# Segment maxima of the attention scores: the mask is added by VectorE from a stored list, not by TensorE from a matmul

## The chip, the cores and the metric

The kernel runs on one core of a Trainium2 chip. The metric is the device time of one execution in microseconds (us). TensorE (PE in the rows) multiplies, VectorE (DVE), ScalarE (ACT) and GpSimd (POOL) work on elements, SyncE (SP) issues most of the DMAs.

## What is computed

Four graph networks run one after the other on the same 3125 nodes and 100,000 edges. What matters here is the first, and in it the loop over four layers. For each layer:

```
Q = ln(h @ Wq);  K = ln(h @ Wk)
score = (Q[src] * K[dst]).sum(-1) + 0.1 * (edge_attr * Q[src][:, :40]).sum(-1) + logm[dst]
smax  = segment_max(score, src)
es    = exp(min(score - smax[src], 20))
denom = segment_sum(es, src)
aggi  = segment_sum((es / (denom[src] + 1e-10)) * (h[dst] @ Wm), src)
h     = ln(h + leaky([h, aggi] @ Wu))
```

Ahead of the layers the same edges pass a gate once (`gate = mlp(edge_attr) + dot(emb[src], adapt emb[dst])`, messages `gate * h[dst] * weight`, summed by `src`).

## The kernel before

Edges were sorted into NB = 25 blocks by source: block i holds the edges whose source is one of the 128 nodes of block i, in KT = 38 tiles of 128 edges. For every tile there is a one-hot list of its sources (`hot_s`, edges by nodes) and its transpose (`hotT_s`, nodes by edges), in fp8, likewise for destinations (`hot_d`, `hotT_d`). The gate's stage (`gate_edges`) makes these lists and stores them to HBM (`rows_src`, `rows_src_t`, `rows_dst`, `rows_dst_t`). The layers' edge stage (`attend`, run four times, 25 blocks each) loads them again for each block.

**The gate's stage** runs over 25 blocks of Q = 7 units. VectorE makes the one-hot lists of the next block in eight chunks, destinations and sources in turn (L1392; a source chunk has 8, 12, 12 and 6 tiles), TensorE transposes them four tiles at a time into PSUM (`turn_hot`, L1290), ScalarE casts them from PSUM into `hotT_s` or `hotT_d` (`copied`, L1347). In the same unit TensorE gathers rows for the current block (`rows`, L1305 and L1307), ScalarE multiplies the embeddings (`emb_in`, L1356), VectorE forms the message (`message`, L1401 to L1409), GpSimd splits it (L1262, L1264), and TensorE sums it (L1317). Every engine's order is written out by hand. In ScalarE's, the casts of a unit stand ahead of its `emb_in`. SyncE's queue stores the lists of a block once all of its casts are done.

**The layers' edge stage** runs over 25 blocks of Q = 4 units of 10, 10, 9 and 9 tiles, several blocks deep. In each unit, in this order on TensorE: the keys and queries of its tiles (`keys`, L1578, L1580), in unit 1 also the turned scores (`turn_scores`, L1588) and the maxima spread over the edges (`maxima`, L1612), then two or three groups of `lay` with `values` (L1622) and `total` (L1633) between them. Ten groups of `lay` make up a block, nine of 4 tiles and one of 2. A group builds in one PSUM bank a table of 128 nodes by up to 512 edges: a first matmul (L1599) puts 0 where the edge belongs to the node and -2^100 where not (`off`, a 128 by 128 constant, times `hotT_s`), then one matmul per tile (L1602) adds the edge's score to every node's row (`sel` times `rows`; in three bf16 parts, so that their sum is exact). VectorE takes the maximum over each row (`top`, L1727). Two PSUM banks take turns, so TensorE starts group x only when VectorE has finished group x - 2.

VectorE's order in a unit: `add` (L1750, unit 1), `scores` (L1709, L1712), `divide` (L1720 to L1722, unit 0), `shifted` (L1744, L1746, unit 1), the unit's two or three `top`, and in unit 0 `largest` (L1734 to L1738). ScalarE takes the scores' rows (L1665), weighs the values (L1688) and copies the keys (L1672), GpSimd adds the attributes (L1536) and splits the values (L1543, L1545). SyncE's queue has for each block i, in this order: `first(i)` (L1498, L1499, waits until the values of block i - 4 are done), `attributes(i)` (L1504) and `last(i - 3)` (L1509, the `hot_s` that `total` needs).

## Time and profile before

| | us |
|---|---|
| median of 3 runs (lowest to highest) | 5786.9 (5772.91 to 5797.48) |
| the profiled execution | 5777.92 |
| its span, first to last instruction | 5776.3 |
| PE busy in the span | 4309.7 (75%) |
| DVE busy | 3791.9 (66%) |
| POOL busy | 2681.4 (46%) |
| ACT busy | 2250.1 (39%) |

Mean granted TensorE clock: 0.816 of full speed. A busy time is the union of an engine's instructions; idle time of an engine that isn't the bottleneck costs nothing. The gate's stage lies from about 1200 to 1866 us, the layers from about 1900 to 4157 us, of them the four edge stages some 430 us each and the rest in smaller stages between them. "Idle before" in a row is time in which the engine waited for the releaser named behind it.

### The profile page before, as it was taken

Reading aid. Unit: us, or ns where it says so; the run is one execution under the profiler, and the core shown is the slowest. Engines: PE = TensorE matmul, PEld = TensorE weight load, DVE = VectorE, ACT = ScalarE, POOL = GpSimd, SP = SyncE. Lnnn points to the kernel's source line nnn. Section 1 sums busy time; section 2 is a strip of 40 time slices with the busy share of each in tenths; the row PEclk is TensorE's granted clock in tenths of the full one; section 3 lists DMA queues with packets and bytes.
Section 4 is the critical chain, followed back from the end, with each engine's and each line's share of the span. In section 5 each row is a group of like instructions: output and inputs, shape, how many; then the busy total and the mean of one; then the engine's idle time right before and its main releaser. Section 6 shows DMA issues by size and latency. Waiting matters only on the chain. (4 is left out here: it accounts for less than half of the span.)

```text
span 5776.3 us, 186815 instructions
## 1 busy us (share of the span) xinstructions
PE 4309.7 (75%) x79576; PEld 3592.7 (62%) x79576; DVE 3791.9 (66%) x7925; ACT 2250.1 (39%) x7746; POOL 2681.4 (46%) x2702
## 2 busy tenths in 40 slices
PE   7999994046666499759976997599757845877887
PEld 4555552035555388748874887488735733877786
DVE  6888875079998588657765785687576446545244
ACT  3333331046666255435543554355401424101310
POOL 2777777756666177517751775277520510000000
PEclk7666665569998699869987998799877977988897
DMA  9322223167775344234423442344255434000000
GB/s 352 74 73 74 70 68 74 42 150 197 195 201 166 113 161 165 92 109 167 154 92 120 157 154 92 123 154 165 80 88 196 158 106 134 2 9 4 4 4 10
DMA packets 488184, 656.80 MB, mean 114 GB/s; under 512 B 316480, under 2 KB 370372, under 8 KB 484117
## 3 DMA queue, kind: packets, MB, share of 16 engines
q1 hardware_dynamic: 450965, 595.00, 32.7%
q0 software_dynamic: 33856, 48.44, 3.4%
q8 instruction: 645, 10.57, 0.7%
q14 instruction: 222, 1.82, 0.1%
q10 hardware_dynamic: 2496, 0.98, 0.1%
HBM read 464.16 MB, written 180.09 MB: 112 GB/s over the span
## 5 line engine op out<-in xcount | busy, mean ns | idle before, releaser
L299 POOL DMA_INDIRECT edges<-sb_bk_rec,sb_bk_pos x782 | 784.8, 1004 | 323.7 <-issue 234.0
L1688 ACT ACTIVATE sb_at_val<-banks,sb_at_prob 128x49 f32<-128x49 f32 x3800 | 776.0, 326 | 189.7 <-PE banks L1622 183.3
L1727 DVE TENSOR_REDUCE sb_at_tops<-banks 128x1 f32<-128x512 f32 x1000 | 652.5, 661 | 279.1 <-PE banks L1602 276.7
L1578 PE MATMUL banks<-sb_near,sb_at_hotT_d 128*128 128x49 bf16 x11100 | 610.3, 184 | 74.0 <-DVE sb_at_key L1709 44.5
L1536 POOL TENSOR_TENSOR sb_at_key<-sb_at_key,sb_at_attr 128x400 f32<-128x400 f32 (+1 forms) x400 | 371.8, 930 | 581.1 <-ACT sb_at_key L1672 489.9
L1580 PE MATMUL banks<-sb_queryp,sb_at_hotT_s 128*128 128x49 bf16 x11400 | 624.5, 185 | 12.8 <-issue 12.3
L1578 PEld LDWEIGHTS banks<-sb_near,sb_at_hotT_d 128*128 128x128 fp8e4 x11100 | 560.3, 96 | 79.1 <-issue 69.3
L1580 PEld LDWEIGHTS banks<-sb_queryp,sb_at_hotT_s 128*128 128x128 fp8e4 x11400 | 559.5, 96 | 15.7 <-issue 15.7
L1543 POOL TENSOR_TENSOR sb_at_val<-sb_at_val 128x490 f32<-128x490 f32 (+1 forms) x400 | 387.4, 968 | 68.9 <-ACT sb_at_val L1688 67.4
L1672 ACT COPY sb_at_key<-banks 128x490 f32<-128x490 f32 (+1 forms) x400 | 225.3, 563 | 462.9 <-PE banks L1580 460.6
L1545 POOL TENSOR_TENSOR sb_at_val<-sb_at_val 128x490 f32<-128x490 f32 (+1 forms) x400 | 386.6, 966 | 31.4
L1622 PE MATMUL banks<-sb_near,sb_at_hotT_d 128*128 128x49 bf16 x11100 | 358.5, 186 | 34.3 <-ACT sb_at_val L1688 22.6
L1602 PE MATMUL banks<-sb_at_rows,sb_sel 114*128 114x128 bf16 x3800 | 379.0, 220 | 1.2 <-issue 1.2
L1599 PE MATMUL banks<-sb_at_hotT_s,sb_off 128*128 128x512 fp8e4 x1000 | 369.4, 369 | 7.3 <-issue 4.5
L1602 PEld LDWEIGHTS banks<-sb_at_rows,sb_sel 114*128 114x128 bf16 x3800 | 297.0, 97 | 116.1 <-issue 9.2
L1622 PEld LDWEIGHTS banks<-sb_near,sb_at_hotT_d 128*128 128x128 fp8e4 x11100 | 331.7, 97 | 43.1 <-ACT sb_at_val L1688 29.1
L1633 PE MATMUL banks<-sb_at_val,sb_at_hot_s 128*128 128x147 bf16 x3800 | 342.3, 237 | 11.9 <-issue 9.1
L1709 DVE TENSOR_TENSOR sb_at_key<-banks,sb_at_key 128x490 f32<-128x490 f32 (+1 forms) x400 | 253.1, 633 | 143.5 <-POOL sb_at_key L1536 143.5
L1262 POOL TENSOR_TENSOR sb_gt_msg<-sb_gt_msg 128x245 f32<-128x245 f32 (+1 forms) x175 | 239.8, 1370 | 189.9 <-DVE sb_gt_msg L1409 189.2
L1633 PEld LDWEIGHTS banks<-sb_at_val,sb_at_hot_s 128*128 128x128 fp8e4 x3800 | 281.1, 101 | 14.4 <-issue 10.7
L2902 PE MATMUL banks<-sb_conv_parts,sb_C 128*128 128x144 bf16 x3750 | 249.3, 232 | 30.8 <-DVE sb_conv_parts L2852 30.8
L2902 PEld LDWEIGHTS banks<-sb_conv_parts,sb_C 128*128 128x128 bf16 x3750 | 247.6, 101 | 31.9 <-DVE sb_conv_parts L2852 31.9
(692 smaller groups left out, 10166.0 us busy)
## 6 DMA issues: line engine op xcount, KB each, us to landing
sb_at_attr<-attr SPq DMA_DIRECT2D x100, 760.0 KB, 7.5
sb_at_hotT_s<-rows_src_t SPq DMA_DIRECT2D x100, 608.0 KB, 3.9
sb_at_hot_s<-rows_src SPq DMA_DIRECT2D x100, 608.0 KB, 8.6
sb_at_hotT_d<-rows_dst_t SPq DMA_DIRECT2D x100, 592.0 KB, 5.9
edges<-sb_pad SPq DMA_DIRECT2D x95, 460.0 KB, 7.0
sb_gt_rec<-edges SPq DMA_DIRECT2D x25, 1748.0 KB
sb_we_hotT<-rows_dst_t SPq DMA_DIRECT2D x52, 592.0 KB, 5.8
attr<-sb_gt_rec SPq DMA_DIRECT2D x25, 760.0 KB, 13.2
```

What stands on the lines that cost most here:

```text
L299: pool.indirect_dma_start(list1, bass.IndirectOffsetOnAxis(pos[:, t:t + 1], 0), rec[:, k, j, :], None).then_inc(sent[k], 16)
L1536: pool.tensor_tensor(key[:, u % 2, 0:n, 0:RBF], key[:, u % 2, 0:n, 0:RBF], attr[:, i % 2, a:b, :], ALU.add).then_inc(s_key, 1)
L1543: pool.tensor_tensor(x[:, 0:n, 1, :], x[:, 0:n, 0, :], halves(0), ALU.subtract).then_inc(s_rest, 1)
L1545: pool.tensor_tensor(x[:, 0:n, 2, :], x[:, 0:n, 1, :], halves(1), ALU.subtract).then_inc(s_split2, 1)
L1578: pe.matmul(ps[:, 0, H1 * j:H1 * j + H1], where, what, start=(n == 0), stop=(n == 2))
L1580: ins = pe.matmul(ps[:, 1 + u % 2, H1 * j:H1 * j + H1], hotT_s[:, i % 4, k, :], queryp[:, i, n, :], start=(n == 0), stop=(n == 2))
L1602: ins = pe.matmul(bank[:, P * j:P * j + P], sel[:, k, :], rows[:, i % 2, :], start=False, stop=(k == ks[-1]))
L1622: ins = pe.matmul(ps[:, 5, H1 * j:H1 * j + H1], where, what, start=(n == 0), stop=(n == 2))
L1633: ins = pe.matmul(ps[:, 6, 0:3 * H1], hot_s[:, i % 2, k, :], high(val[:, v % VB, j].rearrange("p n f -> p (n f)")), start=(k == 0), stop=( ...
L1688: ins = act.mul(val[:, v % VB, j, 0, :], ps[:, 5, H1 * j:H1 * j + H1], prob[:, i % 2, k:k + 1])
L1727: dve.tensor_reduce(tops[:, i % 2, g:g + 1], ps[:, 3 + x % 2, 0:P * len(RG[g])], AX, ALU.max).then_inc(s_top, 1)
L2902: return pe.matmul(ps[:, d % AHEAD, 0:3 * H], C[:, s, P * d:P * d + P], rows(s), start=(s == 0), stop=(s == NB - 1))
```

## The change

TensorE's mask matmul goes from `lay`: each tile's matmul now starts and ends its own accumulation. The mask becomes a stored list, `others` (bf16, 128 nodes by 38 x 128 edges for each block, 1216 KB): 0 where the edge belongs to the node, -2^100 where not. ScalarE makes it in the gate's stage from `hotT_s` (Identity with scale 2^100 and bias -2^100), one activation behind the last cast of each source chunk, four per block. SyncE's queue stores it to HBM behind `hotT_d`. In the layers' edge stage SyncE's queue loads it for block i - 1 behind the attributes of block i and ahead of `last(i - 3)`, into one of two buffers. VectorE's `top` becomes one `tensor_tensor_reduce`: it adds the list to the scores in PSUM, writes the sum to a scratch buffer in SBUF (`left`, f32) and the row's maximum to `tops`.

```diff
 # gate_edges
+    LAST_S = {max(x for x, (t, _, _) in enumerate(TURN) if t == n): (a, b) for n, (side, a, b) in enumerate(MAKE) if side == "s"}
+    others, minus_big = m.sb("gt_others", [P, 2, KT, P], BF16), m.sb("gt_minus_big", [P, 1])
...
                 sp.dma_start(lists["hotT_d"][i], flat(hotT_d, i % 2)).then_inc(s_outt[i % 2], 16)
+                sp.wait_ge(s_others, len(LAST_S) * (i + 1))
+                sp.dma_start(lists["others"][i], flat(others, i % 2)).then_inc(s_outt[i % 2], 16)
...
                 act.copy(hotT[:, i % 2, ks[0]:ks[-1] + 1, :],
                          ps[:, y % 2, 0:P * len(ks)].rearrange("p (k e) -> p k e", e=P), saturate=False).then_inc(s_copied, 1)
+                if x in LAST_S:
+                    a, b = LAST_S[x]
+                    act.wait_ge(s_copied, y + 1)
+                    act.activation(others[:, i % 2, a:b, :], hotT_s[:, i % 2, a:b, :], ACT.Identity, bias=minus_big[:], scale=BIG).then_inc(s_others, 1)
...
 # attend
+            def apart(i):
+                if i >= 2:
+                    sp.wait_ge(s_top, NR * (i - 1))
+                sp.dma_start(flat(others, i % 2), lists["others"][i]).then_inc(s_others[i % 2], 16)
...
                     first(i)
                     attributes(i)
+                if i - 1 < NB:
+                    apart(i - 1)
                 if i >= 3:
                     last(i - 3)
...
                 ks, bank = RG[g], ps[:, 3 + x % 2, :]
-                n = P * len(ks)
-                pe.matmul(bank[:, 0:n], off[:], hotT_s[:, i % 4, ks[0]:ks[-1] + 1, :].rearrange("p k e -> p (k e)"), start=True,
-                          stop=False)
                 for j, k in enumerate(ks):
-                    ins = pe.matmul(bank[:, P * j:P * j + P], sel[:, k, :], rows[:, i % 2, :], start=False,
-                                    stop=(k == ks[-1]))
+                    ins = pe.matmul(bank[:, P * j:P * j + P], sel[:, k, :], rows[:, i % 2, :], start=True, stop=True)
                 ins.then_inc(s_laid, 1)
...
             def top(i, g):
                 x = NR * i + g
+                n, ks = P * len(RG[g]), RG[g]
                 dve.wait_ge(s_laid, x + 1)
-                dve.tensor_reduce(tops[:, i % 2, g:g + 1], ps[:, 3 + x % 2, 0:P * len(RG[g])], AX, ALU.max).then_inc(s_top, 1)
+                if g == 0:
+                    dve.wait_ge(s_others[i % 2], 16 * (i // 2 + 1))
+                if x >= 2:
+                    dve.wait_ge(s_top, x - 1)
+                dve.tensor_tensor_reduce(left[:, x % 2, 0:n], ps[:, 3 + x % 2, 0:n],
+                                         others[:, i % 2, ks[0]:ks[-1] + 1, :].rearrange("p k e -> p (k e)"), 1.0, -BIG,
+                                         ALU.add, ALU.max, tops[:, i % 2, g:g + 1]).then_inc(s_top, 1)
```

## Rows read from the trace of the kernel before

**Rows 1.** By stage: length, busy PE, PEld, DVE, ACT, POOL; clock, DMA share, GB/s.
```profile
2107.02:2296.53 189.51, 183.28 (x5144) 170.47 (x5141) 152.47 (x320) 111.54 (x485) 135.27 (x144) 1.00 0.43 161
1458.00:1562.00 104.00, 68.98 (x1360) 60.93 (x1358) 96.43 (x165) 71.34 (x232) 69.33 (x61) 0.92 0.74 198
```

**Rows 2.** ScalarE's timeline, layers' stage: start, duration; [idle before], at blocks 1 and 12.
```profile
2107.02 0.27 ACT L1665 COPY sb_at_rows<-banks 114x128 bf16<-114x128 bf16 x1 [1.46 <-PE banks L1588]
...
2296.53 0.27 ACT L1665 COPY sb_at_rows<-banks 114x128 bf16<-114x128 bf16 x1 [1.46 <-PE banks L1588]
```

**Rows 3.** Waits from 2107.02 to 2296.53: total us, times, longest.
```profile
DVE sb_at_tops L1727 <- PE banks L1602: 30.0, 60, 2.2
PE banks L1580 <- issue: 2.5, 3, 1.2
PE banks L1578 <- issue: 2.1, 1, 2.1
PE banks L1622 <- issue: 1.6, 4, 0.6
```

**Rows 4.** TensorE's timeline in one unit of the layers' stage.
```profile
2229.05 0.38 PE L1599 MATMUL banks<-sb_at_hotT_s,sb_off 128*128 128x512 fp8e4 x1
2229.27 0.39 PE L1602 MATMUL banks<-sb_at_rows,sb_sel 114*128 114x128 bf16 x4
2229.49 0.77 PE L1622 MATMUL banks<-sb_near,sb_at_hotT_d 128*128 128x49 bf16 x24
...
2230.62 0.85 PE L1633 MATMUL banks<-sb_at_val,sb_at_hot_s 128*128 128x147 bf16 x10
```

**Rows 5.** Groups by shape, VectorE, whole span: busy us, mean ns | idle before.
```profile
L1727 DVE TENSOR_REDUCE sb_at_tops<-banks 128x1 f32<-128x512 f32 x900 | 611.2, 688 | 257.1 <-PE banks L1602 254.7
...
L1709 DVE TENSOR_TENSOR sb_at_key<-banks,sb_at_key 128x490 f32<-128x490 f32 x200 | 131.6, 658 | 129.2 <-POOL sb_at_key L1536 129.2
...
L542 DVE TENSOR_TENSOR_SCAN sb_bk_along<-sb_bk_reset,sb_bk_spill 128x400 bf16<-128x400 bf16 x49 | 48.7, 994 | 1.7
```

**Rows 6.** The same view of ScalarE.
```profile
L2664 ACT ACTIVATE sb_nodes<-sb_C 128x3200 bf16<-128x3200 bf16 x12 | 34.4, 2870 | 20.2 <-PEq L86 19.8
...
L970 ACT ACTIVATE sb_nr_sq<-sb_nr_qk 128x480 f32<-128x480 f32 x20 | 12.0, 602 | 0.6
...
L3233 ACT ACTIVATION_READ_ACCUMULATOR sb_nodes<-banks,sb_wide_cols 108x1 f32 x52 | 10.1, 194 | 0.0
```

**Rows 7.** ScalarE's timeline in the gate's stage: casts of source lists, then embedding products.
```profile
1505.94 0.59 ACT L1347 CAST sb_gt_hotT_s<-banks 128x512 fp8e4<-128x512 f32 x1 [0.28 <-PE banks L1290]
1507.07 1.00 ACT L1356 ACTIVATE sb_gt_emb<-banks,sb_gt_rec 128x32 f32<-128x32 f32 x5 [0.55 <-PE banks L1307]
...
1515.44 1.07 ACT L1347 CAST sb_gt_hotT_s<-banks 128x512 fp8e4<-128x512 f32 x2 [0.24 <-PE banks L1290]
1516.80 1.18 ACT L1356 ACTIVATE sb_gt_emb<-banks,sb_gt_rec 128x32 f32<-128x32 f32 x6 [0.28 <-PE banks L1307]
...
1523.19 1.74 ACT L1347 CAST sb_gt_hotT_s<-banks 128x512 fp8e4<-128x512 f32 x3 [0.20 <-PE banks L1290]
1525.29 1.00 ACT L1356 ACTIVATE sb_gt_emb<-banks,sb_gt_rec 128x32 f32<-128x32 f32 x5 [0.36 <-PE banks L1307]
```

**Rows 8.** VectorE's timeline there: its first operation behind those products.
```profile
1508.11 0.32 DVE L1401 TENSOR_TENSOR sb_gt_prod<-banks,sb_gt_emb 128x160 f32<-128x160 f32 x1
...
1518.63 0.35 DVE L1401 TENSOR_TENSOR sb_gt_prod<-banks,sb_gt_emb 128x192 f32<-128x192 f32 x1
...
1526.81 0.31 DVE L1401 TENSOR_TENSOR sb_gt_prod<-banks,sb_gt_emb 128x160 f32<-128x160 f32 x1
```

**Rows 9.** VectorE's waits from 1300 to 1800 us.
```profile
DVE sb_gt_prod L1401 <- ACT sb_gt_emb L1356: 22.3, 49, 1.3
```

**Rows 10.** DMA issues of the page: count, KB each, median us to landing.
```profile
sb_at_hot_s<-rows_src SPq DMA_DIRECT2D x100, 608.0 KB, 8.6
```

**Rows 11.** The DMA queue's timeline: the block's last load is issued.
```profile
2213.92 0.53 SPq L1509 DMA_DIRECT2D sb_at_hot_s<-rows_src  x1
```

More of the change, by code:

```diff
@@ L1202, in gate_edges @@
     names = ["near", "at", "hot", "turned", "copied", "rows", "emb", "prod", "msg", "rest", "split2", "sum", "added",
-             "link", "second", "back"]
+             "link", "second", "back", "minus", "others"]
     with stage(nc, "gate", *names, *[f"rec{k}" for k in range(HB)], *[f"outh{k}" for k in range(HB)], "outt0", "outt1",
@@ L1206, in gate_edges @@
             block, s_near, s_at, s_hot, s_turned, s_copied, s_rows, s_emb, s_prod, s_msg, s_rest, s_split2, s_sum,
-            s_added, s_link, s_second, s_back, *dmas):
+            s_added, s_link, s_second, s_back, s_minus, s_others, *dmas):
         s_rec, s_outh, s_outt, s_outa, s_far = dmas[0:3], dmas[3:6], dmas[6:8], dmas[8:11], dmas[11:15]
@@ L1247, in _ @@
             for n in range(2):
-                sp.wait_ge(s_outt[n], 32 * ((NB - 1 - n) // 2 + 1))
+                sp.wait_ge(s_outt[n], 48 * ((NB - 1 - n) // 2 + 1))
             sp.wait_ge(s_back, 16)
@@ L1343, in copied @@
                 if x == 0 and i >= 2:
-                    act.wait_ge(s_outt[i % 2], 32 * (i // 2))
+                    act.wait_ge(s_outt[i % 2], 48 * (i // 2))
                     act.wait_ge(s_rows, Q * (i - 1))
@@ L1357, in emb_in @@
                 ins.then_inc(s_emb, 1)
+            act.wait_ge(s_minus, 1)
             for q in range(Q):
@@ L1415, in add @@
                                   ).then_inc(s_added, 1)
+            dve.memset(minus_big[:], -BIG).then_inc(s_minus, 1)
             link(dve.tensor_tensor(tops[:], c["ident"][:, 0:KT], c["ident"][:, KT:2 * KT], ALU.add))
@@ L1441, with attend @@
 K1, KH = H1, 2 * H1
-def attend(nc, c, ps, m, lists, table, near, queryp, dead, sel, off, acc, nmax, spill_dst):
+def attend(nc, c, ps, m, lists, table, near, queryp, dead, sel, acc, nmax, spill_dst):
     TAKE = [range(0, 10), range(10, 20), range(20, 29), range(29, KT)]
@@ L1468, in attend @@
     rows = m.sb("at_rows", [3 * KT, 2, P], BF16)
+    others, left = m.sb("at_others", [P, 2, KT, P], BF16), m.sb("at_left", [P, 2, 4 * P])
     tops = m.sb("at_tops", [P, 2, NR])
@@ L1477, in attend @@
     rings = [f"attr{k}" for k in range(2)] + [f"hots{k}" for k in range(2)] + [f"hotT{k}" for k in range(4)] + [
-        f"far{k}" for k in range(4)] + [f"near{k}" for k in range(Q)]
+        f"far{k}" for k in range(4)] + [f"others{k}" for k in range(2)] + [f"near{k}" for k in range(Q)]
     turned_bank = ps[:, 7, 128:192].bitcast(BF16)
@@ L1482, in attend @@
             s_prob, s_h, s_val, s_rest, s_split2, s_sum, s_added, s_link, *dmas):
-        s_attr, s_hots, s_hotT, s_far, s_near = dmas[0:2], dmas[2:4], dmas[4:8], dmas[8:12], dmas[12:]
+        s_attr, s_hots, s_hotT, s_far, s_others, s_near = dmas[0:2], dmas[2:4], dmas[4:8], dmas[8:12], dmas[12:14], dmas[14:]
         @block.sync
@@ L2524, in first_part @@
             near = t.sb("near", [P, NW, 3, KH], BF16)
-            attend(nc, c, ps, t, lists, table, near, queryp, dead, sel, off, acc, nmax, spill_dst)
+            attend(nc, c, ps, t, lists, table, near, queryp, dead, sel, acc, nmax, spill_dst)
         with ExitStack() as ctx0:
@@ L3466, in network @@
     lists = {"hot_s": nc.dram_tensor("rows_src", [NB, P, KT * P], F8).ap(),
+             "others": nc.dram_tensor("rows_others", [NB, P, KT * P], BF16).ap(),
              "hotT_s": nc.dram_tensor("rows_src_t", [NB, P, KT * P], F8).ap(),
```

## The prediction

> **What bounds the kernel now.** I read the table of busy times by stage first. In the layers' edge stage (the stretch from 2107.02 to 2296.53) TensorE is busy 183.3 of 189.5 us at clock 1.00 (the 2.4 GHz level), VectorE 152.5, GpSimd 135.3, ScalarE 111.5: TensorE sets the pace there [rows 1]. The two ends of the stretch are the same copy, eleven blocks apart, so a block takes 189.51 / 11 = 17.23 us [rows 2]. The waits say the same from the other side: VectorE waits for the laid-out scores, 30.0 us in 60 pieces, while TensorE waits 2.5 + 2.1 + 1.6 = 6.2 us, and for no engine ("issue") [rows 3]. What each would need by itself: TensorE (189.5 - 6.2) / 11 = 16.7 us a block, VectorE (189.5 - 30.0) / 11 = 14.5 us. So any time taken from TensorE counts, but only until VectorE's 14.5 us are reached, and the change puts work just there. In the gate's stage VectorE is busy 96.4 of 104 us, ScalarE 71.3, TensorE 69.0 at clock 0.92, with the DMA engines at a share of 0.74: VectorE sets that pace, and ScalarE isn't far behind it in the order of the work, since VectorE waited for it 22.3 us in 49 pieces within 500 us [rows 1, 9].
>
> **TensorE loses the mask matmul.** In the timeline of one unit the mask's matmul starts at 2229.05, the four tile matmuls behind it at 2229.27, and the next work at 2229.49 [rows 4]. The durations (0.38, 0.39) overlap, so the starts count: 0.22 us for the mask, 0.22 us for the tiles. Nine full groups and one of half the width make 9.5 x 0.22 = 2.1 us a block. TensorE's need falls from 16.7 to 14.6 us, and with the 6.2 / 11 = 0.6 us of its own waits to 15.2 us.
>
> **VectorE's reduce becomes an add with a reduce.** The trace has no such operation. What lies nearest is in two rows: the reduce over 512 elements from PSUM takes 688 ns, and an addition-like operation with one operand in PSUM, one in SBUF and its result in SBUF takes 658 ns for 490 elements, so some 22 elements more bring it to 0.68 us [rows 5]. The pass over the elements should therefore cost what the reduce costs. The maximum has to be brought out beside the sum. The only row for that is ScalarE's read of its accumulator, 194 ns for one element a partition, behind the activation that filled it [rows 6]. I bound the addition by 0 and 0.19 us each and take the middle, 0.1 us, as no row of VectorE decides it: 1.0 us a block. The far bound is the scan, the one two-operand operation here that carries a result from element to element: 994 ns for 400 elements, or 1.27 us for 512 [rows 5]; that is the third rival below. The extra waits in `top` (for the list once a block, for the maximum two groups back on its own engine) cost nothing while the list is there in time.
> The Trainium skill ("VectorE: DVE Perf Modes", section "Two Vector instructions with no wait between them") says that an operation which also writes out its accumulator is two instructions, the main one and an accumulator read. By that rule the sum keeps the second instruction at some price, without it nothing; no row here shows it for VectorE.
>
> **The new period.** VectorE's need becomes 14.5 + 1.0 = 15.5 us, TensorE's 15.2 us. VectorE is then the slightly later one, and its order has two heavy units of four (units 0 and 1 with `divide`, `largest`, `shifted`), in which TensorE, only two groups ahead, has to wait. I add 0.1 us for that: 15.6 us, or 1.6 us less than 17.23. Each of the four layers has 24 full periods; the rest is filling and draining. 96 x 1.6 = 154 us off. If the read costs nothing, TensorE decides at 15.2 us: 96 x 2.0 = 195 us off. With 0.19 us VectorE needs 16.4 us, with the 0.1 us 16.5: 96 x 0.7 = 70 us off.
>
> **ScalarE's four activations a block in the gate's stage.** An activation from SBUF takes 602 ns for 480 elements and 2870 ns for 3200, so (2870 - 602) / 2720 = 0.83 ns an element and 0.2 us ahead of them [rows 6]. Chunks of 1024, 1536, 1536 and 768 elements cost 1.05, 1.48, 1.48 and 0.84 us, 4.9 us a block, and about 0.1 us each for the wait on the cast just issued. ScalarE has the room (71.3 of 104 us), but they stand between the casts and the embedding products on which VectorE waits. Three of the four places are in the rows. The casts end at 1506.53, 1516.51 and 1524.93, and the products start at 1507.07, 1516.80 and 1525.29 [rows 7]. With 0.1 + 1.48, 0.1 + 1.05 and 0.1 + 1.48 us put between, they start at 1508.1, 1517.7 and 1526.5, later by 1.0, 0.9 and 1.2 us. VectorE's first use of them comes 0.04, 0.65 and 0.52 us behind their end (1508.07, 1517.98, 1526.29) [rows 7, 8], and it has its one-hots to make until then. So it is held up 1.0, 0.2 and 0.7 us; for the smallest chunk I take 0.2. That is 2.1 us a block, 24 x 2.1 = 50 us on the stage. The bounds: 20 us, if VectorE gets ahead in the other units, and 4.9 x 25 = 120 us if nothing of it is hidden.
>
> **The DMAs.** The store of 1216 KB a block and its load four times over are new. The layers' stage moved 161 GB/s at a share of 0.43 [rows 1], so 16 engines at that mix would move 374 GB/s, and 1216 KB (1.25 MB) take 3.3 us of them: the share goes to (0.43 x 17.23 + 3.3) / 15.6 = 0.69. In the gate's stage the same 3.3 us in a block of some 26 us (666 us of stage by 25) lift 0.74 to about 0.85. On SyncE's queue the new load stands ahead of `last`, which lands 8.6 us after its issue now [rows 10] and would at 8.6 + 3.3 + 0.5 for the longer queue = 12.4 us. It is issued at 2213.92 and first used by the `total` at 2230.62, 16.7 us later [rows 4, 11]; with a block 1.6 us shorter 15.1 us are left, 2.7 us more than it needs. The list itself lands before that and is wanted at about the same time. I put the DMAs at nothing: the 12.4 us hide beside the other work. If a load were late, it would hold up every block. The new wait in the queue (maxima of block i - 3 done) is met when VectorE has left unit 0, at most a unit after the keys that `attributes` waits for; behind it only `last` is queued.
>
> **The sum.** -154 + 50 = -104 us on the profiled span of 5776.3 us: 5672. The profiled execution took 5777.92 us, 9 below the median of 5786.9, so for the median 5787 - 104 = **5683 us**.
>
> **The rivals.**
> *The gate's stage takes back most of the gain.* ScalarE's work rises from 71.3 / 104 = 0.69 of the time to about 0.83, and it serves TensorE's transposes too, which already wait for its casts. With nothing hidden (+120) and the read at its dear end (-70) the sum is +50; with +95 and -105 it is about -10, 5777 us. For it: the embedding products are late already in 49 cases. Against it: in the rows two of three places have half a microsecond of room. Within half a per cent of no change.
> *The read costs nothing and ScalarE hides.* -195 + 25 = -170: 5617 us. For it: the reduce and the two-operand pass cost alike.
> *The fused operation is slow, and VectorE becomes the bound.* If it runs like the scan, 1.27 us for 0.69, a block costs VectorE 14.5 + 9.5 x 0.58 = 20.0 us, above 17.23: +2.8 x 96 + 50 = +319 us, 6106 us. It decides against the change from 14.5 + 9.5 x d > 17.23, d over 0.29 us, even with the gate's stage at nothing, and with its 50 us from d over 0.23 (0.5 us a block less). A milder form, d = 0.35, gives 17.9 us a block, +64 + 50: 5901 us. For it: only the scan shows feedback with two operands. Against it: the reduce feeds back too, at 688 ns for 512.
> The Trainium skill ("Vector Engine (DVE) Microarchitecture Reference", section "Points that are easy to get wrong") has it that a two-source operation whose sources are both in SBUF and not bf16 runs at half rate, for want of a port to read back its accumulator. Here one source is in PSUM and the other bf16, so by that rule it shouldn't; no row of this trace tells.
> *The change doesn't shorten TensorE's path*, since the tile matmuls were hidden behind the mask's stream: then nothing is gained and 50 us lost. The starts in the rows (0.22 us for each part) speak against it; it goes with the slow cases.
>
> **Chances.** The forecast 0.50, the cheap end 0.18, the gate's stage eating most of it 0.14, slow operation or late load 0.18 (half of it mild). The 80% range goes from 5595 (all of TensorE's time and a hidden ScalarE, -192) to 5830 (the dear read and an unhidden ScalarE, and a little of the mild slow form). A difference under 0.5% (29 us) is about what a measurement can't tell from no change: faster by more than that 0.74, within 0.09, slower 0.17.
>
> **What the profile after would show.** TensorE's group of mask matmuls gone from the layers; the copy of the rows every 15.6 us; `top` at 0.69 us and, if it is there, a row of a second operation near 0.1 us; VectorE's idle before it nearly gone, TensorE waiting for `sb_at_tops`. In the gate's stage ScalarE's four activations at 1.05 to 1.48 us, VectorE's wait for the embedding products up from 22 to some 60 us in 500, and the stage 50 us longer. The forecast falls if `top` takes over 0.9 us, if VectorE's or TensorE's waits name a DMA, or if the gate's stage grows by over 100 us.

## The result

The changed kernel takes 5981.37 us (median of 4 runs, 5965.08 to 5986.14), the kernel before beside it 5782.27 us: a ratio of 1.0337 (95% interval 1.0305 to 1.0368). It is 199 us slower, where 104 us faster was forecast. The two profiled spans differ by 5976.3 - 5776.3 = 200.0 us, and two stages hold all of it.

**The gate's stage.** The view of one tile gives the first and last start of ScalarE's embedding products (ns are min/median/max), of before:

```profile
L1356 ACT ACTIVATE sb_gt_emb<-banks,sb_gt_rec x950: 278/289/385, 1221.8 to 1865.6; 128x32 f32<-128x32 f32 x190
```

and of after, with ScalarE's four new activations a block:

```profile
L1364 ACT ACTIVATE sb_gt_emb<-banks,sb_gt_rec x950: 266/288/316, 1223.0 to 1902.0; 128x32 f32<-128x32 f32 x190
L1356 ACT ACTIVATE sb_gt_others<-sb_gt_hotT_s,sb_gt_minus_big x100: 934/1362/1577, 1208.2 to 1887.8; 128x1536 bf16<-128x1536 fp8e4 x50, 128x1024 bf16<-128x1024 fp8e4 x25, 128x768 bf16<-128x768 fp8e4 x25
```

The stage lasted 643.8 us and lasts 679.0: 35 us longer. VectorE's waits from 1300 to 1800 us, which answer to [rows 9]:

```profile
DVE sb_gt_prod L1410 <- ACT sb_gt_emb L1364: 41.5, 71, 1.3
```

**The layers' edge stage.** From the first copy of the turned scores to the last (24 blocks apart) the four layers took 408.0, 411.7, 410.8 and 410.0 us, in all 1640.5; now they take 450.2, 452.2, 449.2 and 455.7, in all 1807.3. That is 167 us more, and with the gate's 35 us the 200. The rows of after that answer to [rows 1] and [rows 2], for 18 blocks of the first layer (columns as there):

```profile
2097.12:2442.82 345.70, 282.72 (x8232) 278.49 (x8229) 249.70 (x703) 183.96 (x793) 220.55 (x234) 0.93 0.58 209
```

```profile
2097.12 0.27 ACT L1678 COPY sb_at_rows<-banks 114x128 bf16<-114x128 bf16 x1 [6.39 <-PE banks L1605]
...
2442.82 0.27 ACT L1678 COPY sb_at_rows<-banks 114x128 bf16<-114x128 bf16 x1 [6.07 <-PE banks L1605]
```

(2442.82 - 2097.12) / 18 = 19.21 us a block, where the same 18 blocks of before took 17.28 (and the eleven of [rows 2] 17.23). TensorE is busy less (282.7 of 345.7 us; 300.2 of 311.0 in the same 18 blocks of before) and VectorE no more (249.7 us; 249.5): the work of neither fills the block now. The granted clock is 0.93 where it was 1.00. The waits in that stretch, which answer to [rows 3]:

```profile
DVE sb_at_left L1745 <- PE banks L1616: 63.6, 65, 4.7
DVE sb_at_shift L1764 <- PE banks L1625: 21.7, 17, 3.7
PE banks L1635 <- issue: 21.0, 9, 4.3
PE banks L1595 <- issue: 20.2, 13, 3.5
PE banks L1597 <- issue: 18.0, 8, 3.5
PE banks L1616 <- issue: 3.7, 3, 1.5
```

VectorE does wait for TensorE, as before, and more. But TensorE waits for no engine and no list: 21.0 + 20.2 + 18.0 + 3.7 = 62.9 us are "issue", 3.5 us a block, in pieces of up to 4.3 us. Before, the same sum was 10.6 us in 18 blocks, 0.6 a block.

**VectorE's new operation is not the cause.** Its group, beside [rows 5], and two of them in the timeline:

```profile
L1745 DVE CUSTOM_DVE_ANT_0 sb_at_left<-banks,sb_at_others 128x512 f32<-128x512 f32 x900 | 609.0, 687 | 271.4 <-PE banks L1616 262.9 <-issue 1.6
```

```profile
2161.23 0.68 DVE L1745 CUSTOM_DVE_ANT_0 sb_at_left<-banks,sb_at_others 128x512 f32<-128x512 f32 x1
2161.84 0.08 DVE L1745 DVE_READ_ACCUMULATOR2_ANT sb_at_tops<- 128x1 f32 x1
2161.84 0.68 DVE L1745 CUSTOM_DVE_ANT_0 sb_at_left<-banks,sb_at_others 128x512 f32<-128x512 f32 x1
```

It takes 687 ns where the plain reduce took 688. The maximum is brought out by a second instruction of 0.08 us, which lies inside the next one's start: the two additions start 0.61 us apart. The second instruction is what the Trainium skill says ("VectorE: DVE Perf Modes", section "Two Vector instructions with no wait between them"), and the trace agrees; its price here is nothing.

**What TensorE waits for.** Four of its waits, in its own timeline of after:

```profile
2155.26 0.43 PE L1635 MATMUL banks<-sb_near,sb_at_hotT_d 128*128 128x49 bf16 x6 [4.34 <-issue]
...
2170.40 0.20 PE L1595 MATMUL banks<-sb_near,sb_at_hotT_d 128*128 128x49 bf16 x1 [0.85 <-issue]
...
2176.14 0.20 PE L1595 MATMUL banks<-sb_near,sb_at_hotT_d 128*128 128x49 bf16 x1 [1.74 <-issue]
...
2191.53 0.20 PE L1597 MATMUL banks<-sb_queryp,sb_at_hotT_s 128*128 128x49 bf16 x1 [2.03 <-issue]
```

The view of the DMA queues tells packets, MB and share by queue in a stretch. In the 7.5 us from 2145 to 2152.5 these were all:

```profile
q1 hardware_dynamic: 369, 2.28, 74.1%
q0 software_dynamic: 48, 0.08, 9.7%
q14 instruction: 1, 0.01, 0.3%
```

and in the half microsecond behind it there is one packet of 16 KB on the queue q8, which the page calls instruction:

```profile
q8 instruction: 1, 0.02, 12.1%
q1 hardware_dynamic: 5, 0.02, 9.5%
```

TensorE stood still from 2150.9 and went on at 2155.26. The packet itself takes about 1 us of one engine (12.1% of 16 engines in 0.5 us), as it does in the mean with the lists' traffic and without it (65 packets at 1.2% of 16 x 345.7 us here, 1.0 us each; 1.2 us each in experiment 7): it isn't slow, it comes late. Asked in steps of half a microsecond, the view puts the q8 packets at 2144.5, 2152.5, 2156.5, 2161.0, 2167.5, 2173.5, 2177.5, 2182.5 and 2189.0, and so on. Every issue wait of more than 0.8 us between 2150 and 2252 ends 2.2 to 2.9 us behind the start of the half microsecond in which such a packet ran:

| q8 packet at | TensorE goes on at | its wait, us |
|---|---|---|
| 2152.5 | 2155.26 | 4.34 |
| 2167.5 | 2170.40 | 0.85 |
| 2173.5 | 2176.14 | 1.74 |
| 2189.0 | 2191.53 | 2.03 |
| 2202.5 | 2204.95 | 1.14 |
| 2209.0 | 2211.87 | 2.42 |
| 2226.5 | 2228.72 | 2.48 |
| 2240.5 | 2243.36 | 1.09 |
| 2247.5 | 2250.09 | 2.67 |

Packets on that queue in the same 18 blocks, in before:

```profile
q8 instruction: 66, 1.08, 1.3%
```

and in after:

```profile
q8 instruction: 65, 1.06, 1.2%
```

That is 3.6 or 3.7 a block, and the counts fit TensorE's instructions: in after 8232 matmuls and 8229 weight loads (the first two counts of the busy times above), 16461 / 65 = 253 a packet, in before 8413 + 8410 = 16823, 16823 / 66 = 255. TensorE works through one in 311.02 / 66 = 4.7 us at the old pace and would in 15.6 / 3.6 = 4.3 us at the pace that was forecast. While a block's lists are loaded, they come 6 to 9 us apart.

What settles that these are the packets TensorE waits for is where in its stream it waits. From the end of one such wait to the start of the next one, the view of stretches counts its matmuls and weight loads (the first two counts behind the busy times):

```profile
2155.26:2170.35 15.09, 14.29 (x380) 14.18 (x380) 11.82 (x34) 9.52 (x43) 8.19 (x9) 0.83 0.56 192
2170.40:2176.10 5.70, 3.99 (x127) 3.88 (x127) 5.05 (x16) 2.75 (x12) 4.01 (x5) 1.00 0.58 199
2176.14:2191.50 15.36, 13.36 (x381) 13.24 (x381) 10.72 (x27) 7.75 (x33) 9.30 (x10) 0.89 0.69 257
```

That is 760, 254 and 762: with its waits on semaphores counted too, 768, 256 and 768, three packets, one and three. It is so in the whole trace of after: its four layers' edge stages have 133 issue waits of more than 0.8 us, and all 129 distances between neighbours of one stage are a multiple of 256 instructions, give or take one. In before it is so for all 25 distances between 29 such waits. Each of the 133 ends 2.2 to 2.5 us behind the start of a q8 packet. The DMA engines' mean share in slices of 1 us (tenths) shows the loads, of before from 2212 on:

```profile
DMA  0779999981000000000799999941000000004999
```

of after from 2150 on:

```profile
DMA  8310000000005999799996891000003999999999
```

Before, a block's loads fill 7 or 8 slices in a row with a share of 0.5 or more, after, 12; between them lie slices of no share, where a q8 packet such as that at 2156.5 has the engines to itself. So the reading is: TensorE's instructions come over the same DMA engines as the lists, they are late in a long stretch of list traffic, and the extra 1216 KB makes the stretch longer than what TensorE has in store (how much that is, no run measured). The experiments test that.

The Trainium skill ("Runtime: NRT & Kernel Launch", section "Instruction fetch mechanics") says that instructions are refilled in blocks of 16 KiB, 256 of them, over a DMA queue of the sequencer's own, and that this is mostly hidden. The packets and the distances agree with the first (65 packets of 1.06 MB, waits a multiple of 256 instructions apart), and the 3.5 us of waits a block speak against the second.

### The profile page after: what moved, and what is told of

The parts are those of the page before. It is cut to its first block and busy times, and to the rows that moved or that the text cites. A ratio compares the mean times of both kernels' runs of the same rounds, so it can differ in the third digit from the quotient of the medians.

```text
span 5976.3 us, 186953 instructions
## 1 busy us (share of the span) xinstructions
PE 4223.5 (71%) x78491; PEld 3627.4 (61%) x78576; DVE 3811.1 (64%) x8926; ACT 2373.2 (40%) x7846; POOL 2673.5 (45%) x2702
## 5 line engine op out<-in xcount | busy, mean ns | idle before, releaser
L1745 DVE CUSTOM_DVE_ANT_0 sb_at_left<-banks,sb_at_others 128x512 f32<-128x512 f32 x1000 | 649.8, 661 | 339.8 <-PE banks L1616 329.0
L1595 PE MATMUL banks<-sb_near,sb_at_hotT_d 128*128 128x49 bf16 x11100 | 656.0, 188 | 139.3 <-issue 88.9
L1597 PE MATMUL banks<-sb_queryp,sb_at_hotT_s 128*128 128x49 bf16 x11400 | 670.1, 189 | 100.3 <-issue 100.2
L1595 PEld LDWEIGHTS banks<-sb_near,sb_at_hotT_d 128*128 128x128 fp8e4 x11100 | 587.8, 99 | 150.6 <-issue 142.9
L1597 PEld LDWEIGHTS banks<-sb_queryp,sb_at_hotT_s 128*128 128x128 fp8e4 x11400 | 583.9, 98 | 104.8 <-issue 104.7
L1635 PE MATMUL banks<-sb_near,sb_at_hotT_d 128*128 128x49 bf16 x11100 | 384.4, 190 | 98.7 <-issue 69.7
L1635 PEld LDWEIGHTS banks<-sb_near,sb_at_hotT_d 128*128 128x128 fp8e4 x11100 | 356.5, 100 | 116.1 <-issue 79.5
L1616 PE MATMUL banks<-sb_at_rows,sb_sel 114*128 114x128 bf16 x3800 | 397.1, 229 | 40.3 <-issue 30.5
L1646 PE MATMUL banks<-sb_at_val,sb_at_hot_s 128*128 128x147 bf16 x3800 | 369.8, 250 | 2.4 <-POOL sb_at_val L1562 2.1
L1646 PEld LDWEIGHTS banks<-sb_at_val,sb_at_hot_s 128*128 128x128 fp8e4 x3800 | 307.9, 107 | 3.6 <-POOL sb_at_val L1562 3.2
L1616 PEld LDWEIGHTS banks<-sb_at_rows,sb_sel 114*128 114x128 bf16 x3800 | 245.4, 101 | 42.0 <-issue 26.9
L1725 DVE TENSOR_REDUCE sb_at_score<-sb_at_key 128x10 f32<-128x490 f32 (+1 forms) x400 | 255.4, 638 | 13.8
```

The source lines that it names most:

```text
L1595: pe.matmul(ps[:, 0, H1 * j:H1 * j + H1], where, what, start=(n == 0), stop=(n == 2))
L1597: ins = pe.matmul(ps[:, 1 + u % 2, H1 * j:H1 * j + H1], hotT_s[:, i % 4, k, :], queryp[:, i, n, :], start=(n == 0), stop=(n == 2))
L1616: ins = pe.matmul(bank[:, P * j:P * j + P], sel[:, k, :], rows[:, i % 2, :], start=True, stop=True)
L1635: ins = pe.matmul(ps[:, 5, H1 * j:H1 * j + H1], where, what, start=(n == 0), stop=(n == 2))
L1646: ins = pe.matmul(ps[:, 6, 0:3 * H1], hot_s[:, i % 2, k, :], high(val[:, v % VB, j].rearrange("p n f -> p (n f)")), start=(k == 0), stop=( ...
L1745: dve.tensor_tensor_reduce(left[:, x % 2, 0:n], ps[:, 3 + x % 2, 0:n], others[:, i % 2, ks[0]:ks[-1] + 1, :].rearrange("p k e -> p (k e)") ...
```

## The experiments

They ran on three chips, on which before took 5998 us (experiments 1 to 4), 6008 us (5 to 8) and 5773 us (9 to 12). The extra time of the first two lies ahead of the gate's stage (which starts at 1406 to 1422 us in their traces, at 1221 to 1223 in the others) and behind the layers (some 35 us); the layers' edge stages last the same on all. Ratios are to before on the same chip. Forecasts given in microseconds were made for before at 5782, and are read as ratios. The cuts of code leave out the waits that go with a load that is moved or left out.

### 1 and 2: the gate's stage alone, and with the load

```diff
 # e1: the gate's stage of the change, the layers of before
+                    act.activation(others[...], hotT_s[...], ACT.Identity, bias=minus_big[:], scale=BIG)
+                sp.dma_start(lists["others"][i], flat(others, i % 2))
 # e2: the same, and in the layers
+                if i - 1 < NB:
+                    apart(i - 1)
```

> The change's gate stage alone: ScalarE makes the list of 0 and -2^100 and SyncE's queue stores it; the layers are those of before (mask matmul and plain reduce; the list isn't loaded). Theory (the layers' loads do the harm): the gate's stage is about 35 to 55 us longer than before and the layers are unchanged: 5815 to 5845 us, ratio 1.006 to 1.010. Rival (the gate's stage is what made the kernel slower): most of the 200 us is here, above 5900 us.

> As the gate stage alone, and in the layers the list is loaded and waited for as in the change, but nothing reads it: the mask matmul and the plain reduce of before stay. Theory (each block's load lengthens the burst of DMA traffic behind which TensorE's own instructions wait to be fetched, which shows as issue waits): TensorE's issue waits grow from some 60 us to 200 us or more and the time is 150 to 350 us above the gate stage alone, so 5970 to 6180 us, slower than the change itself. Rival (VectorE's new operation does it): no more than 30 us above the gate stage alone.

The gate's stage alone: 1.0065 (1.0041 to 1.0089), its stage 679.3 us long, as in the change, and the layers at 17.30 us a block as before. With the load, which nothing reads: 1.0383 (1.0351 to 1.0416), at least about as slow as the change (the intervals overlap). TensorE does in it what it did before, mask matmul and all, and takes 350.66 / 18 = 19.48 us a block, with 36.6 us of issue waits:

```profile
2291.32:2641.98 350.66, 314.03 (x8413) 289.35 (x8411) 247.06 (x521) 182.86 (x793) 219.48 (x234) 0.96 0.56 206
```

So 3.2% come from the load alone, and VectorE's operation has no part in them. The waits are 1.4 us a block more than in before (2.0 for 0.6), of 2.2 us in all; the other 0.8 is TensorE's busy time (314.0 us for 300.2 on the same instructions), with the granted clock at 0.96 where it was 1.00. So the waits cost clock besides, with more work on TensorE than in the change.

### 3: two loads of the new list a layer

```diff
-                if i - 1 < NB:
+                if i - 1 < 2:
                     apart(i - 1)
```

> The change as it is, but of each layer's 25 loads of the list only the first two are issued, so that blocks 2 to 24 add the list of block 0 or 1 (their maxima are not the reference's). Theory (the load is the harm, the new operation costs what the reduce did): a block takes 15.2 to 15.8 us, TensorE's issue waits are back near 60 us, and the time is 5640 to 5700 us, below before. Rival (VectorE's operation, or its coupling to TensorE, is the bound): within 50 us of the change, 5930 us or more.

Measured 0.9989 (0.9976 to 1.0002). The load is worth 3.5% here too (1.0337 to 0.9989), but the forecast of 15.2 to 15.8 us a block and 60 us of issue waits was wrong: a block takes 16.86 us in the first layer, and TensorE's issue waits there are

```profile
PE banks L1595 <- issue: 17.5, 10, 2.4
PE banks L1635 <- issue: 6.3, 5, 2.0
PE banks L1616 <- issue: 3.9, 3, 1.6
PE banks L1597 <- issue: 2.1, 2, 1.9
```

29.8 us in 18 blocks, 1.7 a block against 0.6 before, with the same bytes as before. A faster TensorE uses up its instructions sooner, so what was enough at 17.3 us a block is no longer. Of the 2.1 us of the mask matmul only 17.30 - 16.86 = 0.4 us came through.

### 4: the load in quarters

```diff
             def apart(i):
-                if i >= 2:
-                    sp.wait_ge(s_top, NR * (i - 1))
-                sp.dma_start(flat(others, i % 2), lists["others"][i]).then_inc(s_others[i % 2], 16)
+                for p, (a, b) in enumerate(PARTS):
+                    if p == 0 and i >= 2:
+                        sp.wait_ge(s_top, NR * (i - 1))
+                    if p:
+                        sp.wait_ge(s_key, Q * i + p + 1)
+                    sp.dma_start(...).then_inc(s_others[4 * (i % 2) + p], 16)
```

> The change with each block's load of the list cut into four parts, issued behind the last load of the block and spaced by TensorE's progress (one part a unit of some 3.8 us) rather than in one burst; same bytes. Theory (the length of the burst without a gap is what starves the instruction fetch): issue waits fall to 60 to 130 us and the time to 5680 to 5800 us. Rival (it is the bytes moved, by load on the DMA engines or on memory, whenever they are moved): no better than 5930 us.

1.0285 (1.0255 to 1.0315), 19.21 us a block, 3.4 us of issue waits. By its numbers the rival would have won, but the experiment didn't do what it was made for: the keys' count stood higher than I had reckoned, the four parts were issued within 6.5 us, and they left the stretch as it was instead of parting it. In its slices, from 2329 on, the loads still fill 11 and 13 slices in a row (12 in the change):

```profile
DMA  4799999998961000000597799999599630000499
```

It tells only that smaller packets and a later place in the queue don't help by much.

### 5 and 6: all loads spaced, in the change and in before

```diff
                     first(i)
-                    attributes(i)
-                if i - 1 < NB:
-                    apart(i - 1)
-                if i >= 3:
-                    last(i - 3)
+                for slot, (loads, pieces) in enumerate([(["attr"], [0]), (["hots"], [1]), ([], [2, 3])]):
+                    sp.wait_ge(s_keys, min(Q * i - 1 + slot, U))
+                    if "attr" in loads and i < NB:
+                        attributes(i)
+                    if "hots" in loads and i >= 3:
+                        last(i - 3)
+                    if i - 1 < NB:
+                        for p in pieces:
+                            apart(i - 1, p)
```

> The change with all of the layers' loads spaced by TensorE's own progress: per block the two transposed lists, then a unit later the attributes and the first quarter of the new list, a unit later the source list and the second quarter, a unit later the rest. Same bytes, four stretches of some 2 to 3 us with gaps where there was one of 12 us. Theory (a long unbroken stretch of data starves the instruction fetch): the stretches are seen apart in the DMA's slices, issue waits fall below 1 us a block, a block takes 15.2 to 16.2 us, ratio to before 0.97 to 0.985. Rival (bytes alone count, wherever they lie): issue waits stay near 3 us a block and the ratio at 1.025 or more.

> The kernel before, with its own loads spaced in the same way and nothing else changed. Theory: its issue waits (0.6 us a block) shrink, ratio 0.990 to 1.000. Rival (bytes alone): 1.000.

The change with spaced loads: 1.0061 (1.0035 to 1.0087), 17.43 us a block, 34.0 us of issue waits in 18 blocks (1.9 a block; 3.5 in the change). Its slices from 2333 on:

```profile
DMA  0599999979933830047999995389834560056999
```

Stretches with a share of 0.5 or more are now 10, 1, 7, 3 and 2 slices long here, with short gaps between. The same bytes in shorter stretches took 2.7% off, so bytes alone aren't it; but it isn't the 15.2 to 16.2 us that I expected either, since at a mean share of 0.67 the gaps are short. Before with spaced loads: 0.9979 (0.9962 to 0.9997), 17.15 us a block, 0.5 us of issue waits, as forecast and hardly to be told from nothing: by this reading, TensorE's store of instructions nearly reached over the loads at before's pace.

### 7: no list traffic

```diff
-                    first(i)
-                    attributes(i)
+                    if i < 4:
+                        first(i)
+                    if i < 2:
+                        attributes(i)
+                if i - 1 < 2:
                     apart(i - 1)
-                if i >= 3:
+                if 3 <= i < 5:
                     last(i - 3)
```

> The change with each list and the attributes loaded only into the first filling of their buffers, so that later blocks work on old lists (the result is not the reference's) and TensorE has next to no data traffic beside its instruction fetch. Theory: issue waits near 0, a block takes 14.7 to 15.4 us, the layers' edge stages are some 190 us shorter than before, ratio 0.97 to 0.98. Rival (the issue waits are TensorE's own, from its shorter matmuls): they stay at 1.5 us or more a block and the ratio near 0.999, as with two loads of the new list.

0.9765 (0.9737 to 0.9792), the gate's 0.65% included. In the first layer, 18 blocks, the length and busy times, TensorE's waits, and the DMA queues:

```profile
2283.31:2559.59 276.28, 268.27 (x8233) 262.71 (x8230) 259.17 (x703) 183.35 (x792) 220.71 (x235) 1.00 0.05 9
```

```profile
PE banks L1627 <- DVE sb_at_mparts L1760: 4.3, 18, 0.2
PE banks L1607 <- DVE sb_at_sparts L1737: 3.7, 18, 0.2
```

```profile
q0 software_dynamic: 864, 1.36, 2.9%
q8 instruction: 65, 1.06, 1.7%
```

Not one issue wait is left, the clock is 1.00, and each block takes 15.3 or 15.4 us, 15.35 in the mean in all four layers. The instruction packets are the same 65, in the mean 276.28 / 65 = 4.25 us apart. Against before, the four layers' edge stages are 1640.5 - 1468.1 = 172 us shorter. Block time and ratio lie in the forecast, and the rival, that the waits come from TensorE's shorter matmuls themselves, is out: its instructions are those of the change. This is the kernel that the prediction described, and it exists only without the lists' traffic (it works on old lists).

### 8: the activation behind the embedding products

```diff
-                if x in LAST_S:
-                    act.wait_ge(s_copied, y + 1)
-                    act.activation(others[...], ...)
 ...
                 emb_in(u)
+                for x in made:
+                    if x in LAST_S:
+                        list_of(j, x)
```

> The spaced loads, and in the gate's stage ScalarE makes the list's part behind the unit's embedding products instead of ahead of them. Theory (the gate's stage grew because VectorE waits for products that stand behind the new activations): the stage is 25 to 45 us shorter than with the activations ahead, ratio 0.005 to 0.007 below the spaced kernel. Rival (the stage grew by the store's DMA traffic): no difference.

1.0065 (1.0045 to 1.0085) against 1.0061 for experiment 5: no difference. The gate's stage is 675.5 us long against 682.9, 7 us and not 25 to 45, and in the other traces with the same gate's stage it is 678.9 to 682.5. VectorE still waits 39.0 us for the products from 1500 to 2000 us, now in 48 longer pieces instead of 47.4 us in 85. So the order on ScalarE isn't what made the stage longer, or not for the most part; the room that ScalarE has lost comes back as a wait wherever the work stands, or the store does it. Which of the two, I haven't tried. TensorE's fetch is not it: its matmuls have 2.8 us of issue waits in that stage of after and 3.8 in before.

### 9 and 10: the mask from the one-hot list that is there

```diff
 # divide: 256 is added to the scores
-                link(dve.tensor_tensor(sp[:, 0, :], score[:, i % 3, :], dead[:, i, :], ALU.add))
+                link(dve.scalar_tensor_tensor(sp[:, 0, :], score[:, i % 3, :], UP, dead[:, i, :], ALU.add, ALU.add))
 # top
+                dve.tensor_tensor_reduce(left[:, x % 2, 0:n], ps[:, 3 + x % 2, 0:n],
+                                         hotT_s[:, i % 4, ks[0]:ks[-1] + 1, :].bitcast(mybir.dt.uint8)..., 1.0 / 56.0, 0.0,
+                                         ALU.mult, ALU.max, tops[:, i % 2, g:g + 1])
 # largest: and taken off the stored maximum again
-                link(dve.tensor_scalar(nm, mp[:, 0:1], 1.0, None, ALU.mult))
+                link(dve.tensor_scalar(nm, mp[:, 0:1], UP, None, ALU.add))
 # e10 besides: the loads spaced as in experiment 6
```

> The mask matmul taken from TensorE as in the change, but without a new list: 256 is added to the scores, VectorE multiplies them by the one-hot list that is in SBUF for TensorE anyway (its fp8 ones read as the byte 56, the product scaled by 1/56) and takes the maximum, 0 standing for the edges of other nodes. No new traffic and nothing new in the gate's stage. Theory: a block takes 16.5 to 16.9 us as with two loads of the new list, issue waits about 1.5 us a block, ratio 0.991 to 0.994. Rival (bytes read by VectorE cost more than bf16): the reduce takes over 0.75 us and the ratio is 1.00 or more.

> The same with the layers' loads spaced by TensorE's progress: the two transposed lists, a unit later the attributes, a unit later the source list. Theory: issue waits under 0.7 us a block, a block takes 15.5 to 16.2 us, ratio 0.975 to 0.985, below both kernels. Rival (spacing helps only where there is much traffic): as without spacing, 0.991 to 0.994.

The mask matmul is gone, no list is made, stored or loaded, and VectorE's operation reads the one-hots' bytes (1.0 is 56 there, hence 1/56): the scores, made positive by 256, are multiplied by 0 or 1 as the maximum is taken. Unspaced: 0.9916 (0.9900 to 0.9931), inside the forecast, though a block takes 17.05 to 17.27 us and not 16.5 to 16.9; the four layers take 1614.1 us, 26 less than before, with 1.9 us of issue waits a block. Spaced: **0.9838 (0.9822 to 0.9855), 5687.4 us against 5772.8**, faster than both kernels. Its first layer's lengths and busy times, TensorE's waits in it, and its operation in the groups of VectorE:

```profile
2058.72:2351.29 292.57, 269.49 (x8233) 264.89 (x8230) 251.50 (x704) 182.01 (x793) 220.85 (x235) 0.99 0.49 171
```

```profile
PE banks L1585 <- issue: 11.4, 9, 2.1
PE banks L1625 <- issue: 6.5, 6, 2.1
PE banks L1606 <- issue: 3.5, 3, 1.4
```

```profile
L1733 DVE CUSTOM_DVE_ANT_0 sb_at_left<-banks,sb_at_hotT_s 128x512 f32<-128x512 f32 x900 | 603.1, 686 | 146.4 <-PE banks L1606 140.9 <-issue 0.2
```

16.25 us a block, clock 0.99, 22.3 us of issue waits in 18 blocks (1.2 a block, where I had expected under 0.7). The four layers take 1542.7 us, 98 less than before. 0.9 us a block are still left to the 15.35 of experiment 7.

### 11 and 12: the change again, and half of its loads

```diff
 # e12
-                if i - 1 < NB:
+                if i - 1 < NB and (i - 1) // 2 % 2 == 0:
                     apart(i - 1)
```

> The change itself, beside the other runs on one chip. Both theories: ratio 1.030 to 1.037.

> The change with the new list loaded for blocks 0, 1, 4, 5, 8, 9 and so on alone; the others add an older one (the result is not the reference's). Theory (each burst that is longer starves TensorE for itself): blocks with the load take some 19 us, blocks without 17, ratio 1.013 to 1.020, half way between two loads (0.999) and the change. Rival (a threshold of traffic): as two loads or as the change.

The change again: 1.0345 (1.0324 to 1.0366). With half of the new list's loads: 1.0171 (1.0150 to 1.0192), half way between 0.9989 and 1.0345, 18.07 us a block and 2.4 us of issue waits (3.5 with all, 1.7 with two). No threshold shows in these three points. The blocks with the load are the long ones: the load comes for two blocks and stays away for two, and block times, taken by their place in that round of four, are 19.0, 17.6, 16.9 and 18.4 us in the mean of the four layers (18.8 to 19.4 in the change).

All of it side by side, first layer, 18 blocks from the fifth copy to the 23rd:

| kernel | ratio | us a block | issue waits a block | clock | DMA GB/s |
|---|---|---|---|---|---|
| before | 1 | 17.28 | 0.6 | 1.00 | 160 |
| the change | 1.034 | 19.21 | 3.5 | 0.93 | 209 |
| e1 gate only | 1.007 | 17.30 | 0.6 | 1.00 | 160 |
| e2 gate and load | 1.038 | 19.48 | 2.0 | 0.96 | 206 |
| e3 two loads | 0.999 | 16.86 | 1.7 | 0.97 | 164 |
| e12 half the loads | 1.017 | 18.07 | 2.4 | 0.94 | 188 |
| e4 quarters | 1.029 | 19.21 | 3.4 | 0.94 | 209 |
| e5 change, spaced | 1.006 | 17.43 | 1.9 | 0.95 | 232 |
| e6 before, spaced | 0.998 | 17.15 | 0.5 | 1.00 | 162 |
| e7 no lists | 0.977 | 15.35 | 0.0 | 1.00 | 9 |
| e9 one-hots | 0.992 | 17.27 | 1.9 | 0.96 | 161 |
| e10 one-hots, spaced | 0.984 | 16.25 | 1.2 | 0.99 | 171 |

In e9 the first layer happened to be the slowest (its others 17.05 to 17.22). In the change a block without its issue waits would take 19.21 - 3.49 = 15.72 us, close to the 15.35 with no traffic. What is left goes with the clock, as far as the rows tell: in the timeline of after, three matmuls of 49 columns take 0.30 us behind the long wait that ends at 2155.26 and 0.23 to 0.24 us from 2162.50 on, and the clock is 0.83 from 2155.26 to 2170.35 (the row above).

## Why the prediction was wrong

**TensorE's loss of the mask matmul** (2.1 us a block; need 14.6 us, 15.2 with its own waits): right in kind, 0.3 us too much. In experiment 7 TensorE is busy 268.27 / 18 = 14.9 us a block, where its need before was 16.7: 1.8 us came.

**VectorE's operation** (0.68 us and 0 to 0.19 for the read): right in the pass, 687 ns, and too dear in the read. The range began with the right end, 0. So VectorE didn't become the later engine: in experiment 7 TensorE is busy 268.3 of 276.3 us and sets the pace. That its 15.35 us lie so near the forecast's 15.6 (172 us off the layers for 154) is partly luck: the 15.6 held 1.0 us of reads that cost nothing, and the 15.35 hold none of the 0.6 us of issue waits that TensorE's 15.2 were reckoned with.

**VectorE's lateness in its heavy units**: 0.1 us was added, and experiment 7 leaves TensorE 4.3 + 3.7 us of waits for VectorE in 18 blocks, 0.4 a block. They stand before the turned scores (L1607) and the maxima (L1627), not before the tables of `lay`, and are inside the 15.35.

**ScalarE's activations**: 1.05, 1.48 and 0.84 us forecast, 1.15, 1.58 and 0.94 us measured (1575 ns for 1536 elements, 1148 for 1024, 935 for 768). 50 us were forecast for the stage and 35 came. The mechanism given for it, products held up behind the new activations, didn't hold by itself: with the activations behind the products the stage was 3 to 7 us shorter, not 35.

**The DMAs**: here the prediction failed. "I put the DMAs at nothing: the 12.4 us hide beside the other work" was reckoned against the first user of each list, and those users are indeed not late. The landing times came nearly as forecast (the page of after; count, KB, us to landing; 12.4 us was the forecast for the second):

```profile
sb_at_others<-rows_others SPq DMA_DIRECT2D x100, 1216.0 KB, 10.9
sb_at_hot_s<-rows_src SPq DMA_DIRECT2D x100, 608.0 KB, 11.7
```

and in the 18 blocks of the rows above no engine's wait names a list. What was left out is another user of the same DMA engines that isn't in the kernel's text: TensorE's instruction fetch. The sum had 6.2 us of its issue waits [rows 3] and carried them over as a constant, 0.6 us a block. They were the sign of it. They grow with the length of the load stretches (0.6 to 2.0 us a block, experiment 2) and with TensorE's pace (0.6 to 1.7, experiment 3), and the change raised both: 3.5. In the layers -154 us became +167. Experiment 7 has the change's instructions there without the lists' traffic, and lies 167 + 172 = 339 us below it: that is what the traffic costs through TensorE's waits and clock. The term put at nothing, with the 0.6 us a block (58 us) that was carried over, stood for these 339 us; the other terms were 18 us (the layers' pace) and 15 us (the gate's stage) too dear.

**The rivals.** None was this one. "Slow operation or late load" had 0.18, but its mechanism was VectorE's price; the sentence that a late load would hold up every block had the right engines and the wrong waiter. The chance of slower, 0.17, was too low, because the one resource that the change loads most, the DMA engines, was checked only for deadlines.

**What the profile after should have shown**: `top` at 0.69 us with a second operation near 0.1 us, and VectorE's waits for the products up to about 60 us (41.5), came. The copy every 15.6 us and TensorE waiting for `sb_at_tops` did not: TensorE's issue waits took that place, which the list of signs didn't hold.

**What stays open.** That TensorE waits for its instructions rests on the places of its waits, a multiple of 256 instructions apart, on their ends behind the packets of one queue, and on their going when the list traffic goes. The number of TensorE's instructions was never changed by itself. Why a packet comes 6 to 9 us after the last one under load (asked for late, or held up in a queue), how far ahead TensorE fetches, and whether an order of the queues could let a packet pass, no run tells. Nor was the gate's 35 us split between ScalarE's time and the store.

## What to carry to other kernels

Before moving work off TensorE at the price of DMA traffic, look at TensorE's waits for "issue" and at the instruction queue's packets: this kernel, unrolled into many short matmuls, lives on a steady fetch, and both a longer stretch of data (experiment 2) and a faster TensorE (experiment 3) starved it. Reckon traffic not only against the deadline of its own reader but for how long it fills the engines without a gap, and space the loads by TensorE's own progress. A mask that is already in SBUF in another form (here one-hots, with an offset that makes the scores positive) costs no traffic at all: it was worth 0.8% by itself and 1.6% with the loads spaced, where the new list lost 3.4%.

## What the runs showed of the hardware

- The fused add-and-maximum over 512 elements, one operand in PSUM and one bf16 in SBUF, takes 687 ns, the same as the plain maximum; with a byte operand, 686 ns. Bringing the maximum out is an instruction of 0.08 us that costs the next one nothing (0.61 us from start to start).
- TensorE's instructions come in packets of 16 KB, 3.6 for a block. They came 4.25 us apart in the mean with no list traffic, and 6 to 9 us apart during a stretch of list loads, though one takes about 1 us either way. TensorE's 133 issue waits of more than 0.8 us in the change's layers lie a multiple of 256 instructions apart and end 2.2 to 2.5 us behind the start of a packet.
- The granted clock fell with TensorE's waits: 0.93 with 3.5 us of waits in 19.21 us, 1.00 with none in 15.35 us, on the same instructions. In experiment 2 it fell to 0.96 with the instructions of before, which ran at 1.00.
- Two chips took 3.9 and 4.1% longer than the third for the kernel before (5998 and 6008 against 5773 us), 185 to 200 us of it ahead of the gate's stage and some 35 us behind the layers.
